# Cross-attention layer with an FP6 last layer: the last layer from f16 parts, small VectorE operations with two tensor operands, projection ahead of the turn

## The reference

```python
x = x + xattn(layernorm(x), ctx, mask, Wq, Wk, Wv, Wo, bo, g1, b1, g2, b2)
xn = layernorm(x)
# mx_quantize: scale = max(max|block of 32| / 7.5, 1e-30); q = nearest FP6 E2M3 value of block / scale
xd = dequantized(mx_quantize(xn));  wd = dequantized(mx_quantize(weight))
x = x + xd @ wd.T + bias
```

## Time and profile before

| | us |
|---|---|
| median of 3 runs | 4335.55 |
| lowest and highest | 4334.62, 4340.15 |
| the profiled execution's own time | 4338.36 |
| its span, first to last instruction | 4336.6 |

### The profile page before, as it was taken

The page is one execution under the profiler, slowest core; times in us unless marked ns, Lnnn a source line. Parts: engine busy times, 40 slices in busy tenths (PEclk is TensorE's granted clock), DMA queues, the critical chain, the costliest instruction groups (busy, mean ns, idle before and its releaser), DMA issues.

```text
span 4336.6 us, 87951 instructions
## 1 busy us (share of the span) xinstructions
PE 4204.9 (97%) x36752; PEld 1392.0 (32%) x35088; DVE 3454.3 (80%) x3960; ACT 2857.8 (66%) x5193; POOL 2938.9 (68%) x1830
## 2 busy tenths in 40 slices
PE   4999999999999999999999999999999999999999
PEld 2322243222532234222342223422234222342223
DVE  5689767887678976888768897688976899768986
ACT  3388843888438875488755886558865588646885
POOL 3199752996529965399644996449963599536994
PEclk9999999999999999999999999999999999999999
DMA  5256652666426574265733567335664356643664
GB/s 201 73 118 128 141 172 64 121 124 152 158 61 124 120 185 131 61 129 117 205 109 70 118 127 195 104 75 121 125 190 109 80 118 125 185 113 78 122 131 117
DMA packets 191558, 541.68 MB, mean 125 GB/s; under 512 B 29025, under 2 KB 103073, under 8 KB 148786
## 3 DMA queue, kind: packets, MB, share of 16 engines
q0 software_dynamic: 43776, 318.79, 36.7%
q1 hardware_dynamic: 147378, 217.27, 16.2%
HBM read 119.37 MB, written 22.05 MB: 33 GB/s over the span
## 4 chain that ended last, share of the span: by engine, by line
PE 76%; DVE 8%; POOL 6%; DMA 5%; ACT 3%; issue 2%; SPq 0%; DVEq 0%; ACTq 0%; POOLq 0%
PE banks L1212 18%; PE banks L1111 18%; PE banks L1224 17%; PE banks L1175 7%; PE banks L1179 5%; DVE max_parts L689 5%; PE banks L1255 4%; PE banks L1105 4%; POOL wkT_wvT_wqT L474 3%; PE banks L1080 3%; DMA sums<-wkT_wvT_wqT 3%; ACT region L979 2%; POOL wdT L474 1%; DMA region<-in_x 1%; DMA wdT<-wkT_wvT_wqT 1%
## 5 line engine op out<-in xcount | busy, mean ns | idle before, releaser
L689 DVE TENSOR_REDUCE max_parts<-banks 128x2 f32<-128x1024 f32 x2048 | 2403.3, 1219 | 364.9 <-PE banks L1175 340.8
L979 ACT ACTIVATE region<-banks 128x512 f32<-128x512 f32 x4096 | 2190.1, 610 | 428.9 <-PE banks L1212 360.8
L474 POOL TENSOR_TENSOR wkT_wvT_wqT<-region 128x1024 f32<-128x1024 f32 x528 | 1353.4, 2776 | 451.6 <-ACT region L979 341.1
L1212 PE MATMUL banks<-queries_stacked,keys_stacked 98*32 98x512 f16 x16384 | 1270.4, 382 | 13.3 <-ACT values L963 6.2
L1224 PE MATMUL banks<-region,values 128*32 128x512 f32 x8192 | 1080.2, 600 | 19.1 <-ACT region L979 15.5
L1212 PEld LDWEIGHTS banks<-queries_stacked,keys_stacked 98*32 98x32 f16 x16384 | 403.4, 95 | 1168.0 <-ACT region L979 770.5
L1111 PE MATMUL banks<-region,wkT_wvT_wqT 128*128 128x512 f16 x2304 | 558.0, 381 | 15.1 <-DMA wkT_wvT_wqT<-weights_split 12.8
L1175 PE MATMUL banks<-keys_stacked,queries_stacked 33*128 33x512 f16 x2432 | 475.1, 387 | 6.8 <-DVE max_parts L689 3.5
L474 POOL TENSOR_TENSOR sums<-region 128x1024 f32<-128x1024 f32 x144 | 386.1, 2826 | 0.2 <-ACT region L979 0.2
L454 POOL TENSOR_TENSOR region<-row_sums_inverse,region 128x512 f16<-128x512 f32 x80 | 93.1, 1163 | 432.5 <-ACT region L942 431.8
L1111 PE MATMUL banks<-wkT_wvT_wqT,region 128*128 128x512 f16 x1536 | 368.8, 380 | 0.0
(11 more groups left out here) (108 smaller groups left out, 3354.0 us busy)
## 6 DMA issues: line engine op xcount, KB each, us to landing
wdT<-wkT_wvT_wqT POOLq DMA_DIRECT2D x96, 1024.0 KB, 12.0
wkT_wvT_wqT<-wkT_wvT_wqT POOLq DMA_DIRECT2D x80, 1024.0 KB, 7.5
sums<-wkT_wvT_wqT POOLq DMA_DIRECT2D x72, 1024.0 KB, 7.5
wkT_wvT_wqT<-sums POOLq DMA_DIRECT2D x40, 1024.0 KB, 7.6
wkT_wvT_wqT<-weights_split SPq DMA_DIRECT2D x8, 3072.0 KB, 20.8
keys_stacked<-region SPq DMA_DIRECT2D x384, 64.0 KB, 2.0
keys_stacked<-sums SPq DMA_DIRECT2D x384, 64.0 KB, 2.0
region<-in_x SPq DMA_DIRECT2D x16, 1024.0 KB, 8.3
```

Of the source, the lines that this page charges most:

```text
L474: e.tensor_tensor(SUMS[dst][:, half], PR[i][:, half], PR[i + 1][:, half], ALU.add).then_inc(s_pr, 1)
L689: e.tensor_reduce(mpart[:, buf, :, a, t, c], MXB[parity], AX.X, ALU.max).then_inc(s_mxd, 1)
L979: e.activation(PR[u % 4][:, j * HALF:j * HALF + HALF], score_bank(m % NU, kt, j)[0], ACT.Exp, scale=SCALE).then_inc(s_ex, 1)
L1212: mm = e.matmul(dst[HD * t:HD * t + HD, :], KA[0:STR, ds(ka + (j * C + (u + 1) * P + HD * t), HD)], QA[0:STR, ds(qa[j], HALF)], start=True ...
```

## The change

The last layer's weights and its turned input are kept as high and low f16 parts. ACT's copy now writes the high part, and a new DVE operation, `turned_low(k)`, reads the turned bank and the high part and writes the low one; a new semaphore s_tr counts it, and turns, products and SP's store of the weights wait for it instead of for ACT's copy. The product is `contract_split`, and y_tile divides by 64. In the prologue the four turned tiles have a bank each, and DVE makes their low parts after L665. In DVE's round i, `turned_low(i-2)` stands after `quantise(i-1)` and ahead of `parts[1]` and `y_tile(i-3)`. For k below 4, PE takes `out_project(k+4)` ahead of `turn_quantised(k)`. DVE's `block_scales` and the four-element variance become `scalar_tensor_tensor` with a constant tile as second tensor. The next batch's first chunk's statistics move to rounds 3 and 4, POOL's next_rstd(0) to after round 4, and ACT's centring to rounds 5 and 6.

```diff
@@ -82,7 +82,7 @@
     CALLS_FIRST = XCH
-    NEXT_AT = (2, T // P - 1)
+    NEXT_AT = (4, T // P - 1)
     CALLS = CCH + T // P + len(NEXT_AT)
@@ -140,7 +140,8 @@
         XD = [V[:, D * i:D * i + D] for i in range(2)]
-        XDT = [V[:, D * (2 + i):D * (3 + i)].rearrange("p (c t) -> p c t", c=CC) for i in range(2)]
+        XDT = [V[:, D * (2 + i):D * (3 + i)].bitcast(F16).rearrange("p (s c t) -> p s c t", s=2, c=CC) for i in range(2)]
+        WDP = split(WD[:, :, :].rearrange("p c d -> p (c d)"))
         RL = sb("row_sums_inverse", [P, HALF], F32)
@@ -161,6 +162,8 @@
         mhalf = sb("minus_half", [P, 4], F32)
+        least = sb("least_scale", [P, NB], F32)
+        eps_once, eps_twice = (sb(f"eps_{n}", [P, 4], F32) for n in ("once", "twice"))
         mpart = sb("max_parts", [P, 2, 2, 2, QT, 4], F32)
@@ -218,6 +221,7 @@
         s_cst = sem("constants_set")
+        s_le = sem("least_values_set")
         s_msk = sem("mask_steps")
@@ -270,6 +274,7 @@
         s_tc = sem("quantised_copied")
+        s_tr = sem("quantised_low_part")
         s_ff = sem("ffn_done")
@@ -300,7 +305,7 @@
             tokens(0, x_chunks(0)[:, 0])
-            e.wait_ge(s_tc, 4)
+            e.wait_ge(s_tr, 4)
             e.dma_start(wd_dram, SUMS[4]).then_inc(s_fs, 16)
@@ -418,6 +423,8 @@
                 e.memset(spare[:, i:i + 1], 0.0).then_inc(s, n)
+            for t, value in ((least, FP8_STEP * SCALE_MIN), (eps_once, EPS), (eps_twice, EPS * EPS)):
+                e.memset(t[:, :], value).then_inc(s_le, 1)
             e.memset(mhalf[:, :], -0.5).then_inc(s_pr, 2)
@@ -598,12 +605,11 @@
                 ch.settle()
-                if twice:
-
-
-                    e.tensor_scalar(var, mean_var[:, :, 1], 1 + EPS, EPS * EPS, ALU.mult, ALU.add).then_inc(s_ve, 1)
+                if var.shape[1] == 1:
+                    e.tensor_scalar(var, mean_var[:, :, 1], EPS, None, ALU.add).then_inc(s_ve, 1)
                 else:
-                    e.tensor_scalar(var, mean_var[:, :, 1], EPS, None, ALU.add).then_inc(s_ve, 1)
+                    e.scalar_tensor_tensor(var, mean_var[:, :, 1], 1 + EPS if twice else 1.0,
+                                           (eps_twice if twice else eps_once)[:, :], ALU.mult, ALU.add).then_inc(s_ve, 1)
@@ -648,6 +654,7 @@
+            e.wait_ge(s_le, 3)
             e.wait_ge(s_wf, 48)
@@ -665,6 +672,11 @@
                                    ALU.mult, ALU.subtract).then_inc(s_wol, 1)
+
+            for n in range(4):
+                e.wait_ge(s_tc, n + 1)
+                e.scalar_tensor_tensor(WDP[:, 1, :, n * P:n * P + P], PS[:, n, :].rearrange("p (c t) -> p c t", c=CC),
+                                       W_SCALE, WDP[:, 0, :, n * P:n * P + P], ALU.mult, ALU.subtract).then_inc(s_tr, 1)
@@ -863,8 +875,8 @@
                     ch.settle()
-                    ch.did(e.tensor_scalar(scale64[i % 2][:, :], amax[:, :], FP8_STEP / FP6_MAX, FP8_STEP * SCALE_MIN,
-                                           ALU.mult, ALU.max))
+                    ch.did(e.scalar_tensor_tensor(scale64[i % 2][:, :], amax[:, :], FP8_STEP / FP6_MAX, least[:, :],
+                                                  ALU.mult, ALU.max))
@@ -879,7 +891,13 @@
                     e.wait_ge(s_fb, b * TT + i + 1)
-                    e.tensor_tensor(X1[:, i, :], bank(4 + i % 2), X1[:, i, :], ALU.add).then_inc(s_y, 1)
+                    e.scalar_tensor_tensor(X1[:, i, :], bank(4 + i % 2), 1.0 / W_SCALE, X1[:, i, :],
+                                           ALU.mult, ALU.add).then_inc(s_y, 1)
+
+                def turned_low(k):
+                    e.wait_ge(s_tc, 4 + b * TT + k + 1)
+                    e.tensor_tensor(XDT[k % 2][:, 1], bank(2 + k % 2).rearrange("p (c t) -> p c t", c=CC),
+                                    XDT[k % 2][:, 0], ALU.subtract).then_inc(s_tr, 1)
@@ -906,12 +924,14 @@
                         last_part()
+                    if 2 <= i <= TT + 1:
+                        turned_low(i - 2)
                     if i == TT + 1:
...
                         y_tile(i - 3)
-                    if 1 <= i <= NEXT_AT[0]:
+                    if NEXT_AT[0] - 1 <= i <= NEXT_AT[0]:
                         next(parts[0], None)
@@ -924,8 +944,8 @@
                 e.wait_ge(s_tt, n + 1)
-                e.activation(WD[:, :, n * P:n * P + P], PS[:, n % 2, :].rearrange("p (c t) -> p c t", c=CC),
-                             ACT.Copy).then_inc(s_tc, 1)
+                e.activation(WDP[:, 0, :, n * P:n * P + P], PS[:, n, :].rearrange("p (c t) -> p c t", c=CC),
+                             ACT.Copy, scale=W_SCALE).then_inc(s_tc, 1)
             e.wait_ge(s_wof, 16)
@@ -1054,14 +1074,14 @@
                             e.wait_ge(s_ff, b * TT + k - 1)
-                        e.activation(XDT[k % 2], bank(2 + k % 2).rearrange("p (c t) -> p c t", c=CC),
+                        e.activation(XDT[k % 2][:, 0], bank(2 + k % 2).rearrange("p (c t) -> p c t", c=CC),
                                      ACT.Copy).then_inc(s_tc, 1)
...
                                      scale=rs1[i % 2][:, :]).then_inc(s_nz, 1)
-                    if i in (4, 5) and b + 1 < B:
-                        centred(0, (i - 4) * 2, 2)
+                    if NEXT_AT[0] < i <= NEXT_AT[0] + 2 and b + 1 < B:
+                        centred(0, (i - NEXT_AT[0] - 1) * 2, 2)
@@ -1083,10 +1103,8 @@
                 e.wait_ge(s_xd, n + 1)
-                if n >= 2:
-                    e.wait_ge(s_tc, n - 1)
-                turn(bank(n % 2), lambda c: XB[0][:, n, c * P:c * P + P]).then_inc(s_tt, 1)
-            e.wait_ge(s_tc, 4)
+                turn(bank(n), lambda c: XB[0][:, n, c * P:c * P + P]).then_inc(s_tt, 1)
+            e.wait_ge(s_tr, 4)
             e.wait_ge(s_w, 16 * 3)
@@ -1363,17 +1381,17 @@
                     if k >= 2:
-                        e.wait_ge(s_tc, 4 + b * TT + k - 1)
+                        e.wait_ge(s_tr, 4 + b * TT + k - 1)
                     turn(bank(2 + k % 2), lambda c: XD[k % 2][:, c * P:c * P + P]).then_inc(s_tt, 1)
...
                 def ffn(k):
-                    e.wait_ge(s_tc, 4 + b * TT + k + 1)
+                    e.wait_ge(s_tr, 4 + b * TT + k + 1)
                     if k >= 2:
...
                         e.wait_ge(s_fl, b * 16 + 16)
-                    contract(bank(4 + k % 2), lambda cc: XDT[k % 2][:, cc, :],
-                             lambda cc: WD[:, cc, :]).then_inc(s_ff, 1)
+                    contract_split(bank(4 + k % 2), lambda s, cc: XDT[k % 2][:, s, cc, :],
+                                   lambda s, cc: WDP[:, s, cc, :], iter(()), iter(())).then_inc(s_ff, 1)
@@ -1382,8 +1400,8 @@
                     if k < LEAD:
+                        out_project(k + LEAD)
                         turn_quantised(k)
-                        out_project(k + LEAD)
                     if k == TT - 2:
```

## The result

The changed kernel takes 4396.3 us (median of 4 runs, 4393.9 to 4404.2), the kernel before 4336.3 (4 runs): ratio 1.0138, 95% interval 1.0125 to 1.0151. It is slower by 60 us, where the prediction said 4383, 47 more than before, with a range up to 4396.0. The direction and most of the places were right; the loss was forecast a fifth too small (47 of 60 us), and the measured median lies 0.3 us outside the range. The four runs alone lie 10 us apart, so on which side of the edge it fell is chance; the 13 us between forecast and measurement are not.

The account below looks back on a forecast made before the run. PE is busy 97% of the span, but from tile 4 of each tail it waits, with DVE's rounds at 5.02 us. Tails 41, last batch 2 and start 4 made 47 us on 4338.4, carried to the median: 4383, range 4360 to 4396.

Parts of the forecast that it names:

- Projection, turn, copy, low part, product as one chain: Tail, tiles 0 to 2: 7.33 us a tile against 6.46, PE idle some 1.6 between turn and product.
- Low part 7 ahead of the second chunk's statistics: DVE's queue at the batch's turn: GpSimd waits for the variance, PE idles some 4.5 us; costs 3.2 per transition.
- The tails: First output projection to next batch's first projection: 63.24 us against 57.37, 5.9 more per transition.
- The start: Prologue: SP waits for four low parts, so levels and first projection come later: +4 us, bounds +1.6 and 6.6.
- The hold of small operations: DVE's two-tensor scale stays held by GpSimd: 4383, chance 0.55; rival, it is freed: 4376, chance 0.2.
- Costed at nothing: Next tokens' statistics two tiles later on DVE: no cost, since waits at low parts 1 and 2 cover them.
- I walk both orders with the same durations: Method for the tail: old and new order walked with identical instruction durations, 0.05 to 0.1 us between engines.
- Last batch, +2: Last tail, nothing following: y of tile 7 ends 2.1 us later, counted as +2 us.
- Tails, 41: Seven transitions between batches at 5.9 us each: +41 us.
- Behind the first projection, nothing: Stretches between a first projection and the following tail: the forecast had no added time there.
- From the profiled execution to the median: Whole kernel: profiled 4338.4 us lies 2.8 above the median 4335.6; the 47 us were carried to the median.

Follow-up runs that it names:

- PE kept busy: Changed kernel plus identity turns on PE, six ahead of product 0 and eight ahead of the next batch's first projection: 4388.1 us, ratio 1.0112.
- the statistics ahead alone: Changed kernel with the second chunk's statistics put ahead of the low part of tile 7 in DVE's round 9: 4361.0 us, ratio 1.0056.
- both edits: Changed kernel with the second chunk's statistics ahead of low part 7 and PE's turn k ahead of projection k + 4: 4324.1 us, ratio 0.9969.

## Why the prediction was wrong, and where it was right

- **Projection, turn, copy, low part, product as one chain.** Right: 7.21 us from turn 1 to turn 2 and on, forecast 7.33; PE idle 1.4 between turn and product, forecast 1.6. Undone, it is worth 35 us.
- **Low part 7 ahead of the second chunk's statistics.** Right in place and mechanism: GpSimd waits 3.16 us for the variance and PE 4.35, forecast 4.5. Undone, 35 us: 21 was forecast as queue, and the seven tails are 21.7 shorter. The rest lies behind them, where the fifteen matmuls are at full clock again (11.4) and all that follows starts with earlier statistics; the run changes both, and does not part them.
- **The tails.** 63.1 - 57.0 = 6.05 us per transition, forecast 5.9; in batch 0 64.4 instead of 63.2, by 1.4 of slow clock in product 0. That the mean fits is partly luck: without the slow clock of two of the seven tails (3.1 us) the growth is 5.6. The five tails without slow product 0 take 62.2 to 63.2 us, so the walk was up to 1.0 long.
- **The start.** +3.4, forecast +4. The cause is SP's order, as said: the levels are issued 6.8 us later (45.14 against 38.35). But they land 3.7 us after their issue, where the forecast had 4.4 and the kernel before 7.2. In the kernel before, a load of 1 MB of tokens (36.96) and the 1 MB store (37.59) both stood just ahead of them; now the load has been issued 8 us earlier and only the store is near. Moving the store gave 5.95, since the levels are then issued 7.1 us earlier (38.01) and take 4.8 to land.
- **The hold of small operations.** Right: the two-tensor form is held like the other (1.28 and 1.12 against 0.18), and putting it back changes nothing. The Trainium skill's rule that the prediction leaned to ("SBUF — State Buffer", section "Who interferes with whom": two SBUF inputs contend with a GpSimd instruction that reads SBUF) agrees with this trace; the reading by which only one-tensor forms are held falls.
- **"Costed at nothing": the statistics' new place.** Wrong, without harm to the sum. The step read "DVE's waits at low parts 1 and 2 cover them"; true of rounds 3 and 4, but at the old place, rounds 1 and 2, they wait for a load and delay low part 0, which no wait covers. The move in this change is worth 17 us, about half of them by the clock, without which the result would have been 4416. It made no error in the sum, since the walk was of the new place.
- **The step that failed: one duration for each of PE's instructions, whatever stood before it.** "I walk both orders with the same durations" priced all of PE's work from rows at full clock. The walk itself gave PE waits of 4.5 and 3 us that it did not have before, and did not ask what they do to the clock. The terms that came out too small by it:
  - *Last batch, +2*: measured 4.2, of which 1.7 is product 0 at the slow clock.
  - *Tails, 41*: measured 42.4, of which 3.1 is slow clock in two product 0.
  - *Behind the first projection, nothing*: measured 5.6. The fifteen matmuls take 11.4 us more in seven transitions, and PE's waits in these stretches fall by 5.1. How much of the 5.6 would be gone without the slow clock stays open: with PE kept busy the fifteen matmuls are fast again, the medians fall by 11 us, but the stretches of the profiled execution are as long as before (477.2 us for 477.1), with 15 us more of waiting for the row sums.
- **From the profiled execution to the median.** The prediction took off 2.8 us, by which the profile before stood above the median (2.1 with the fourth run); the one after stands 2.3 below its own. The 47 us became 55.5 in the spans and 60 in the medians. These 4.4 us between spans and medians are chance, and they made the difference between inside and outside the range.

What stays open: why the stretches between the tails are 475.0 us in the versions with the second chunk's statistics ahead, 476.4 in the kernel before, 477.1 in the changed one and 477.2 with PE kept busy. All end with the product that needs the transfer of the row sums; PE waits for it 4.5 us in all with the statistics ahead alone, 2.9 with both edits, 6.2 in the kernel before, 3.6 in the changed kernel and 18.8 with PE kept busy. So PE is not always what sets their length. Why the transfer itself comes later there, no run tells.

## What to carry to other kernels

When work is moved to another engine's queue, walk the queue behind it as well: here one subtraction of 0.7 us, placed ahead of four statistics, cost as much as taking away the work that hid a copy. A step that waits for the end of a chain belongs behind everything that doesn't. And where a walk gives TensorE a wait of several us that it did not have, price what follows at the lower clock too. Filling such a wait gave full clock behind it here, but the clock then fell in other places, and the gain was 11 us in one version and none in another, where another wait stood behind the slow product. Taking the wait of 4.35 us away gave 35.

## What the runs showed of the hardware

- The granted clock fell to half after PE's wait of 4.35 us before the next batch, in each of seven transitions, and not after 1.4 us between turn and product. Between these the wait does not decide alone: product 0 of the changed kernel was slow behind 3.00, 3.03 and 2.44 us, and at full clock behind 3.08, 2.60, 2.47 and twice 2.23. In the run with PE kept busy, product 4 ran at the slow clock behind 2.03 us of idle time, in the changed kernel behind 2.04 at full clock in 2.75:

```profile
593.92 0.66 PE L1100 MATMUL banks<-ident,values 128*128 128x128 f32 x4 [2.04 <-POOL values L573]
594.41 2.75 PE L1129 MATMUL banks<-wdT,values 128*128 128x512 f16 x12
```

- Twelve f16 matmuls of 128x512 took 2.75 us at 2.4 GHz, 5.30 where the clock was slow for all of them (granted 0.50 from 567.18 to 572.48, statistics at their old place), and 3.92 to 4.45 where it was slow for a part.
- A small DVE instruction with two tensors in SBUF is held by GpSimd for the rest of its addition, just as a one-tensor one is: 16 elements per partition took 174 to 1289 ns in one form and 174 to 1290 in the other, in the same kernel.
- A 2 KB transfer was landed and used 7.2 us after its issue where a load and a store of 1 MB each had been issued less than 1.4 us ahead of it, 4.8 where only the load had, and 3.7 where only the store had (the load 8 us earlier). The 32 KB mask row stood between in each case.
